# Reading two ids straight from device memory, and issuing their factors ahead of the small vectors and of x

## The chip, the cores and the metric

The kernel runs on one core of a Trainium2 chip. The metric is the device time of one execution in microseconds; three runs of the kernel before are given. A core has five engines with queues of their own: TensorE (PE, with its weight loads PEld), VectorE (DVE), ScalarE (ACT), GpSimd (POOL) and SyncE (SP). DMAs are issued here from the queues of SP and ACT (SPq, ACTq in the profile), and once from that of GpSimd.

## What is computed

x is 8 batches of 256 tokens of 128 features. Each batch has an expert id (0 to 7) and a language id (0 to 3). Cut to what matters:

```python
# first half, x: (8, 256, 128)
h = relu(x @ wi.T + 2 * lora(x; common) + 2 * lora(x; experts[id]))      # 128 -> 512
y = h @ wo.T + 2 * lora(h; common) + 2 * lora(h; experts[id])            # 512 -> 128
for r in range(4):                                                       # 4 rounds
    cw = softmax of the two largest of 4 gate logits (cur @ Wg[r] + bg[r])
    cur = cur + sum_e cw[e] * (gelu(cur @ W1[e] + b1[e]) @ W2[e] + b2[e])
x = x + cur
# second half
z = lora(x; language id) + embed[language id]
x = x + w3(gelu(h2(gelu(h1(silu(w1 z) * (w2 z))))))                      # each with a scale per row
```

## The kernel before

Tokens run along the free dimension, features along the partitions: x is (128, 2048), cut into four chunks of 512 tokens, two batches each. Every fp32 operand is split into a high and a low part of type fp32r, and a product is three matmuls (line 503: high x high, high x low, low x high).

The first stage makes, for each batch, its own weights: the common and the expert's factors are multiplied on TensorE (`merge_group`, lines 511 to 530), VectorE adds twice the product to the base weights (`merged_sum`, line 1029), ScalarE makes the high part (line 798), GpSimd or VectorE the low part (lines 417 and 1034). Kind 0 is the input matrix, kind 1 the output matrix. The factors of a batch are 64 rows of `lora_all`, picked by its id. Then `cond_hidden` and `cond_out` apply the merged weights batch by batch; then come four rounds of 16 expert steps, and the second half.

How the start is ordered. All orders are written out by hand, one program per engine, with semaphores between them.

- SP (line 345): it loads the 16 ids into SBUF (`ids`, line 346), then the small vectors (`vec`, line 347, and the gate bias `gbias`, line 348). It waits for the ids, reads the id of batch 0 into a register (line 244), and issues the two halves of batch 0's factors (`first_load`, line 257); then in the same way the whole factors of batch 2 (`lora_load`, line 247), x of chunk 1 (line 262), batches 4 and 5, x of chunks 2 and 3, batches 6 and 7, the mixture's weights (line 361) and the language factors.
- ACT (lines 893 to 901): base weights of kind 0 (line 265), x of chunk 0 (line 262), a small activation that brings in its table (line 896), a wait for the ids, the factors of batch 1 (`first_load`) and of batch 3 (`lora_load`), base weights of kind 1; then `x0_high(0)` (line 876), the high part of chunk 0's x, and the high parts of the merged weights.
- VectorE (from line 1217): `split_gate`, which waits for both small vectors (line 1200) and splits the gate's weights in four operations (lines 1201 to 1209); `x0_low(0)` (line 1016), which waits for x0_high(0); the sums (0,0) and (1,0), `first_low` (line 1034), the sums (0,1), (1,1), (2,0), (3,0), (2,1), (3,1) (batch, kind).
- TensorE (from line 673): 13 warm-up matmuls on a zero tile (line 590), merge_group 0 (batches 0 and 1, kind 0; waits for the first halves of their factors) and 1 (the same batches, kind 1; second halves), two more warm-up matmuls, merge_group 2 and 3 (batches 2 and 3), cond_hidden(0), cond_hidden(1), and so on.

A PSUM bank is written again only after VectorE's sum has read it: merge_group 3 writes the banks of the sums (0,0) and (1,0), and cond_hidden(1) the banks of the sums (2,0) and (3,0). An fp32 matmul shows as two instructions in the profile, so the 13 warm-up matmuls are 26 rows.

Of the kernel before, what the change touches and what calls it, by code (L numbers as in the profile page):

```python
# [31 lines left out]
LORA_EXPERTS, LANGS = 8, 4  # L32
# [79 lines left out]
def adaln_ffn(nc, x_t, batch_ids, cond_base, lora_all, lang_lora, lang_embed,  # L112
              moe_w, vecs, gate_bias, ffn_w, out_t):
    ctx = ExitStack()
    with ctx:
        def sb(name, shape, dt):
            return ctx.enter_context(nc.sbuf_tensor(name, shape, dt))
# [31 lines left out]
        ids = sb("ids", [1, 2 * BATCHES], I32)  # L149
# [73 lines left out]
        def lora_rows(b, kind):  # L223
            first = 2 * RANK * (2 * (b % 2) + kind)
            return slice(first, first + 2 * RANK)
# [15 lines left out]
            return max([SUMS.index(MERGED[i]) + 1 for i in range(k) if merge_bank(i) == at], default=0)  # L241

        def lora_expert(queue, b):
            return queue.value_load(ids[0:1, b:b + 1], min_val=0, max_val=LORA_EXPERTS - 1)  # L244

        def expert_load(queue, b, e):
            queue.dma_start(lora[4 * RANK * (b % 2):4 * RANK * (b % 2 + 1), b // 2, :],
# [2 lines left out]
        def lora_load(queue, b):  # L250
            expert_load(queue, b, lora_expert(queue, b))

        def first_load(queue, b):

            e = lora_expert(queue, b)
            for kind, arrived in enumerate((lora_in[b], first_out_in[b])):
                queue.dma_start(lora[lora_rows(b, kind), 0, :],  # L257
                                lora_all[bass.ds(e, 1), 2 * RANK * kind:2 * RANK * (kind + 1), :]
                                .rearrange("e r n -> (e r) n")).then_inc(arrived, 16)

        def x_load(queue, c):
            queue.dma_start(x0[:, c, :], x_t[:, c * CHUNK:(c + 1) * CHUNK]).then_inc(x_in[c], 16)

        def base_load(queue, kind):
            queue.dma_start(base[:, kind, :], cond_base[:, kind, :]).then_inc(base_in[kind], 16)
# [42 lines left out]
        def out_parts(c):  # L308

            parts = 2 if c == CHUNKS - 1 else 1  # L310
            return [slice(i * CHUNK // parts, (i + 1) * CHUNK // parts) for i in range(parts)]
# [25 lines left out]
        def store_out(queue, c, t):  # L337
            queue.dma_start(out_t[:, c * CHUNK:(c + 1) * CHUNK][:, t], x0[:, c, t]).then_inc(out_done, 16)
# [5 lines left out]
        @block.sync  # L344
        def _(sp):
            sp.dma_start(ids[:], batch_ids).then_inc(ids_in, 16)
            sp.dma_start(vec[:], vecs).then_inc(small_in, 16)
            sp.dma_start(gbias[:], gate_bias.to_broadcast([SQ, ROUNDS * EXPERTS])).then_inc(small_in, 16)  # L348
            sp.wait_ge(ids_in, 16)
            first_load(sp, 0)  # L350
            lora_load(sp, 2)
            x_load(sp, 1)
            for b in (4, 5):
                lora_load(sp, b)
            for c in (2, 3):
                x_load(sp, c)
            for b in (6, 7):
                lora_load(sp, b)
            for i in (0, 2, 1, 3):
                half = slice((i % 2) * 2 * F, (i % 2 + 1) * 2 * F)  # L360
                sp.dma_start(moe_raw[:, i // 2, half], moe_w[:, i // 2, half]).then_inc(moe_in[i], 16)
            for b in range(BATCHES):
                e = sp.value_load(ids[0:1, BATCHES + b:BATCHES + b + 1], min_val=0, max_val=LANGS - 1)
                sp.dma_start(lang_f[b // 4][:, b % 4, :],
                             lang_lora[bass.ds(e, 1), :, :].rearrange("e r n -> (e r) n")).then_inc(lang_in, 16)
                sp.dma_start(emb[:, b:b + 1],
                             lang_embed[bass.ds(e, 1), :].rearrange("e d -> d e")).then_inc(lang_in, 16)

            def store_gate(slot, turned, read, stored):

                sp.wait_ge(cw_turned, turned)
                if read is not None:
                    sp.wait_ge(cw_ready[slot], read)
                sp.dma_start(cw_dram[slot:slot + 1, :].rearrange("s (e t) -> (s e) t", t=CHUNK),
                             cw_row[0:EXPERTS, :])\
                  .then_inc(cw_stored, 16)
                sp.wait_ge(cw_stored, stored)

            def broadcast_gate(slot):

                sp.dma_start(cw_all[:, slot, :, :].rearrange("p e t -> p (e t)"),
                             cw_dram[slot:slot + 1, :].to_broadcast([P, EXPERTS * CHUNK])).then_inc(cw_ready[slot], 16)

            for slot in range(2):
                store_gate(slot, slot + 1, None, 16 * slot + 16)
                sp.wait_ge(moe_lo_done, max(MOE_ORDER.index(EXPERTS * slot + e) for e in range(EXPERTS)) + 1)
                broadcast_gate(slot)
            with sp.Fori(1, ROUNDS * CHUNKS // 2) as pair:

                read = sp.to_reg(16 * pair)  # L390
                counts = [(sp.to_reg(2 * pair + slot + 1), sp.to_reg(32 * pair + 16 * slot + 16),
                           sp.to_reg(2 * EXPERTS * pair + EXPERTS * (slot - 1) + ADD0)) for slot in range(2)]
                for slot, (turned, stored, gated) in enumerate(counts):
                    store_gate(slot, turned, read, stored)
                    sp.wait_ge(add_done, gated)
                    broadcast_gate(slot)
            for c in range(CHUNKS - 1):
                sp.wait_ge(evac_done, Z_ALL + c + 1)
                store_out(sp, c, slice(0, CHUNK))
            sp.wait_ge(out_done, 16 * sum(len(out_parts(c)) for c in range(CHUNKS)))  # L400
# [391 lines left out]
        def _(act):  # L792
# [98 lines left out]
                   .then_inc(moe_hi_done, 1)  # L891

            base_load(act, 0)
            x_load(act, 0)
            act.wait_ge(const_done, 1)
            act.activation(low_any[0:1, :], blank[0:1, 0:1], ACT.Gelu_apprx_tanh)
            act.wait_ge(ids_in, 16)
            first_load(act, 1)
            lora_load(act, 3)
            base_load(act, 1)  # L900
            x0_high(0)
# [460 lines left out]
```

## Time and profile before

| | us |
|---|---|
| three runs: median (lowest, highest) | 484.4 (484.19, 484.8) |
| span of the profiled execution, first to last instruction | 482.6 |
| median less that span | 1.8 |
| TensorE busy | 477.5 |
| ScalarE busy | 393.6 |
| VectorE busy | 387.7 |
| GpSimd busy | 116.9 |

The profile is that of one execution; its own time with what lies around the span isn't listed, so the span is set beside the median of the runs. A row of the timeline gives the start and the length in us, the engine, the line of the kernel, the operation, the tile written and the tiles read, how many instructions are merged in the row, and in brackets the idle time of the engine just before it with what ended it. A row marked SPq or ACTq is an instruction of a queue's sequencer, such as the issue of a DMA. The landing of a DMA is counted from the start of its issue. The granted clock of TensorE is 1.00 in every stretch that the profile lists.

### The profile page before, as it was taken

The numbers are of one execution on the slowest core, as the hardware profiler recorded it, in microseconds if no ns is written. First come the engines' busy times: TensorE is split into PE (matmuls) and PEld (weight loads), VectorE is DVE, ScalarE is ACT, GpSimd is POOL, SyncE is SP. The second block draws the span as 40 slices with busy tenths as digits, with TensorE's granted clock in tenths as the row PEclk, the third lists the DMA queues.
The fourth block names the chain that finished last, engine by engine and source line by source line (L and its number), as shares of the span: only waits on it lengthen the run. The fifth ranks groups of instructions, "written<-read, shape, count | busy, mean of one in ns | idle before, by whom it ended". The sixth has DMA issues, their size and how long they took to land.

```text
span 482.6 us, 7478 instructions
## 1 busy us (share of the span) xinstructions
PE 477.5 (99%) x2270; PEld 396.2 (82%) x2270; DVE 387.7 (80%) x641; ACT 393.6 (82%) x542; POOL 116.9 (24%) x99
## 2 busy tenths in 40 slices
PE   8999999999999999999999999999999999999997
PEld 7998888888888888888888888888888887888886
DVE  4889899998889898988898898889897658554343
ACT  4889988888788898888888888888888888697653
POOL 3995212121212212121212121231313144400000
PEclk9999999999999999999999999999999999999999
DMA  7702702020210202020202112120202000000002
GB/s 206 219 6 90 282 2 89 0 90 1 88 52 35 88 0 88 0 88 0 88 1 87 37 50 87 45 89 0 88 2 88 2 0 0 1 0 1 0 22 70
DMA packets 7179, 26.31 MB, mean 55 GB/s; under 512 B 2226, under 2 KB 2610, under 8 KB 4978
## 3 DMA queue, kind: packets, MB, share of 16 engines
q1 hardware_dynamic: 5970, 21.73, 12.8%
q0 software_dynamic: 288, 2.88, 1.6%
q10 hardware_dynamic: 896, 1.38, 1.0%
q8 instruction: 14, 0.23, 0.2%
q14 instruction: 11, 0.09, 0.1%
HBM read 24.81 MB, written 1.18 MB: 54 GB/s over the span
## 4 chain that ended last, share of the span: by engine, by line
PE 97%; DMA 1%; SPq 1%; DVE 0%; issue 0%
PE bank L505 34%; PE bank L506 34%; PE bank L509 26%; PE bank L594 1%; PE bank L595 1%; DMA stage<-lora_all 1%; PE bank L527 1%; PE bank L524 0%; SPq L244 0%; PE bank L540 0%; SPq L257 0%; DVE act_out L1029 0%; DVE stage L1029 0%; DVE x L1280 0%; SPq L348 0%
## 5 line engine op out<-in xcount | busy, mean ns | idle before, releaser
L812 ACT ACTIVATE act_out<-bank,vec 128x512 f32<-128x512 f32 x256 | 165.4, 682 | 41.7 <-PE bank L509 32.2
L1119 DVE TENSOR_TENSOR hid_lo<-act_out,hid_hi 128x1024 fp32r<-128x1024 f32 x128 | 156.7, 1243 | 33.2 <-ACT hid_hi L817 33.1
L817 ACT ACTIVATE hid_hi<-act_out 128x1024 fp32r<-128x1024 f32 x128 | 135.9, 1062 | 8.0 <-PE bank L509 0.2
L468 POOL TENSOR_TENSOR cur<-cur,prod 128x512 f32<-128x512 f32 x48 | 64.9, 1353 | 237.1 <-DVE prod L1130 236.6
L505 PE MATMUL bank<-hid_hi,moe_hi 128*128 128x512 f32 x256 | 99.9, 390 | 0.0
L505 PE MATMUL bank<-xhi,moe_hi 128*128 128x512 f32 x256 | 99.7, 390 | 0.0
L509 PE MATMUL bank<-hid_hi,moe_lo 128*128 128x512 f32 x256 | 99.7, 390 | 0.0
L506 PE MATMUL bank<-hid_lo,moe_hi 128*128 128x512 f32 x256 | 99.7, 389 | 0.0
L506 PE MATMUL bank<-xlo,moe_hi 128*128 128x512 f32 x256 | 99.6, 389 | 0.0
L509 PE MATMUL bank<-xhi,moe_lo 128*128 128x512 f32 x256 | 99.6, 389 | 0.0
L505 PEld LDWEIGHTS bank<-hid_hi,moe_hi 128*128 128x128 f32 x256 | 48.1, 188 | 11.3 <-issue 0.2
L509 PEld LDWEIGHTS bank<-hid_hi,moe_lo 128*128 128x128 f32 x256 | 48.1, 188 | 10.2
L506 PEld LDWEIGHTS bank<-hid_lo,moe_hi 128*128 128x128 f32 x256 | 48.1, 188 | 10.1
L509 PEld LDWEIGHTS bank<-xhi,moe_lo 128*128 128x128 f32 x256 | 48.0, 188 | 10.0
L505 PEld LDWEIGHTS bank<-xhi,moe_hi 128*128 128x128 f32 x256 | 48.1, 188 | 10.0
L506 PEld LDWEIGHTS bank<-xlo,moe_hi 128*128 128x128 f32 x256 | 48.1, 188 | 9.9
L1130 DVE SCALAR_TENSOR_TENSOR prod<-bank,vec,cw_all 128x512 f32<-128x512 f32 x64 | 47.5, 742 | 0.2 <-PE bank L509 0.2
L505 PE MATMUL bank<-hid_hi,ffn_hi 128*128 128x512 f32 (+1 forms) x108 | 37.8, 353 | 0.0
L506 PE MATMUL bank<-hid_lo,ffn_hi 128*128 128x512 f32 (+1 forms) x108 | 37.4, 350 | 0.0
L999 ACT ACTIVATE act_out<-bank,vec 128x512 f32<-128x512 f32 x32 | 21.3, 685 | 14.5 <-PE bank L506 14.3
L505 PE MATMUL bank<-xhi,ffn_hi 128*128 128x512 f32 (+1 forms) x84 | 29.8, 355 | 0.5 <-DVE act_out L1029 0.5
L506 PE MATMUL bank<-xlo,ffn_hi 128*128 128x512 f32 (+1 forms) x84 | 29.3, 349 | 0.0
(125 smaller groups left out, 566.3 us busy)
## 6 DMA issues: line engine op xcount, KB each, us to landing
cw_all<-cw_dram SPq DMA_DIRECT2D x16, 1024.0 KB, 4.7
stage<-ffn_w POOLq DMA_DIRECT2D x1, 2304.0 KB, 8.6
cw_all<-moe_w SPq DMA_DIRECT2D x4, 512.0 KB, 7.8
stage<-lora_all SPq DMA_DIRECT2D x5, 160.0 KB, 3.7
x<-x_t SPq DMA_DIRECT2D x3, 256.0 KB, 4.3
out_t<-x SPq DMA_DIRECT2D x3, 256.0 KB, 2.5
cur<-cond_base ACTq DMA_DIRECT2D x2, 256.0 KB, 3.3
stage<-ffn_w POOLq DMA_DIRECT2D x1, 512.0 KB, 4.0
```

What stands on the lines that cost most here:

```text
L468: pool.tensor_tensor(cur[:, c, :], cur[:, c, :], prod[:, s % 2, :], ALU.add).then_inc(add_done, 1)
L505: pe.matmul(out, w_hi, r_hi, start=start, stop=False)
L506: mm = pe.matmul(out, w_hi, r_lo, start=False, stop=stop and w_lo is None)
L509: return pe.matmul(out, w_lo, r_hi, start=False, stop=stop)
L527: mm = pe.matmul(bank[:, at, fc * D:(fc + 1) * D], factors[:, fc * P:(fc + 1) * P], factors[:, F:F + D], start=True, stop=True)
L594: pe.matmul(bank[0:SQ, at, :], wg_now[:], xhi[:, c, :], start=True, stop=False)
L595: pe.matmul(bank[0:SQ, at, :], wg_now[:], xlo[:, c, :], start=False, stop=True).then_inc(logit_done, 1)
L812: act.activation(act_out[:, f // 2, f % 2, :], bank[:, f, :], ACT.Gelu_apprx_tanh, bias=vec[:, V_B1 + e * FC + f:V_B1 + e * FC + f + 1]).t ...
L817: act.activation(hid_hi[:, s % 2, 2 * pr:2 * pr + 2, :], act_out[:, pr, :, :], ACT.Copy)\
L999: act.activation(act_out[:, o // 2, o % 2, :], bank[:, o + FC * (at % 2), :], ACT.Gelu, scale=vec[:, v + o:v + o + 1]).then_inc(gelu_done, 1)
L1119: dve.tensor_tensor(hid_lo[:, s % 2, 2 * pr:2 * pr + 2, :], act_out[:, pr, :, :], hid_hi[:, s % 2, 2 * pr:2 * pr + 2, :].bitcast(F32), ALU ...
L1130: dve.scalar_tensor_tensor(prod[:, s % 2, :], bank[:, 4 + s % 2, :], vec[:, V_B2 + e:V_B2 + e + 1], cw_all[:, c % 2, e, :], ALU.add, ALU.m ...
```

## The change

The id of batches 0 and 1 is read into a register from the input tensor in device memory, not from its copy in SBUF, so that this read needs no wait. SP issues batch 0's factors right after the ids' own transfer, ahead of `vec` and `gbias`, and ACT issues batch 1's ahead of x of chunk 0. All other ids are still read from SBUF after the wait. Bytes, transfers and arithmetic are the same.

```diff
         def lora_expert(queue, b):
-            return queue.value_load(ids[0:1, b:b + 1], min_val=0, max_val=LORA_EXPERTS - 1)
+
+            where = batch_ids if b < 2 else ids
+            return queue.value_load(where[0:1, b:b + 1], min_val=0, max_val=LORA_EXPERTS - 1)
...
         @block.sync
         def _(sp):
             sp.dma_start(ids[:], batch_ids).then_inc(ids_in, 16)
+            first_load(sp, 0)
             sp.dma_start(vec[:], vecs).then_inc(small_in, 16)
             sp.dma_start(gbias[:], gate_bias.to_broadcast([SQ, ROUNDS * EXPERTS])).then_inc(small_in, 16)
             sp.wait_ge(ids_in, 16)
-            first_load(sp, 0)
             lora_load(sp, 2)
             x_load(sp, 1)
...
             base_load(act, 0)
+            first_load(act, 1)
             x_load(act, 0)
             act.wait_ge(const_done, 1)
             act.activation(low_any[0:1, :], blank[0:1, 0:1], ACT.Gelu_apprx_tanh)
             act.wait_ge(ids_in, 16)
-            first_load(act, 1)
             lora_load(act, 3)
             base_load(act, 1)
             x0_high(0)
```

## Rows read from the trace of the kernel before

**Rows 1.** The page: the span, and busy time with its share of it.

```profile
span 482.6 us, 7478 instructions
PE 477.5 (99%) x2270; PEld 396.2 (82%) x2270; DVE 387.7 (80%) x641; ACT 393.6 (82%) x542; POOL 116.9 (24%) x99
```

**Rows 2.** Stretches: length, TensorE busy (instructions), granted clock, DMA share, GB/s.

```profile
8.00:12.30 4.30, 3.65 (x36) 1.00 0.87 251
...
50.00:470.00 420.00, 419.97 (x1859) 1.00 0.12 45
```

**Rows 3.** Waits of TensorE over the span: us in total, times, longest.

```profile
PE bank L505 <- DVE act_out L1029: 0.5, 1, 0.5
PE bank L524 <- DMA stage<-lora_all: 0.2, 1, 0.2
```

**Rows 4.** Timeline of TensorE, 0 to 14 us: start, length, line, operation.

```profile
1.06 5.45 PE L590 MATMUL bank<-blank 128*128 128x128 f32 x26 [1.06 <-POOL blank L405]
6.44 0.70 PE L524 MATMUL bank<-stage 32*128 32x512 f32 x2
...
9.02 1.16 PE L527 MATMUL bank<-stage 32*128 32x128 f32 x16
...
12.29 0.36 PE L505 MATMUL bank<-xhi,ffn_hi 128*128 128x256 f32 x1 [0.50 <-DVE act_out L1029]
```

**Rows 5.** Timeline of VectorE, 0 to 14 us.

```profile
4.84 0.17 DVE L1201 COPY wg_raw<-vec 128x16 f32<-128x16 f32 x1 [4.84 <-DMA gbias<-gate_bias]
...
5.52 0.18 DVE L1209 CAST wg_now<-wg 128x32 fp32r<-128x32 f32 x1
6.41 0.69 DVE L1016 TENSOR_TENSOR xlo<-x,xhi 128x512 fp32r<-128x512 f32 x1 [0.71 <-ACT xhi L876]
7.67 1.29 DVE L1029 SCALAR_TENSOR_TENSOR prod<-bank,cur 128x512 f32<-128x512 f32 x2 [0.57 <-PE bank L527]
...
11.47 0.68 DVE L1029 SCALAR_TENSOR_TENSOR act_out<-bank,cur 128x512 f32<-128x512 f32 x1
```

**Rows 6.** Timeline of ScalarE and its queue, 0 to 14 us.

```profile
1.25 0.45 ACTq L262 DMA_DIRECT2D x<-x_t  x1
...
2.92 0.37 ACTq L257 DMA_DIRECT2D stage<-lora_all  x1
...
5.11 0.59 ACTq L265 DMA_DIRECT2D cur<-cond_base  x1
5.75 0.63 ACT L876 ACTIVATE xhi<-x 128x512 fp32r<-128x512 f32 x1 [2.52 <-issue]
```

**Rows 7.** Timeline of SP's queue, 0 to 14 us.

```profile
0.81 0.36 SPq L346 DMA_DIRECT2D ids<-batch_ids  x1
...
1.65 0.42 SPq L348 DMA_DIRECT2D gbias<-gate_bias  x1
3.09 0.85 SPq L257 DMA_DIRECT2D stage<-lora_all  x2
4.71 0.58 SPq L247 DMA_DIRECT2D stage<-lora_all  x1
```

**Rows 8.** Register loads, line 244: ns min/median/max, first and last start.

```profile
L244 SPq TENSOR_LOAD <-ids x6: 268/273/480, 2.1 to 10.9; - x6
...
L244 ACTq TENSOR_LOAD <-ids x2: 287/380/472, 2.0 to 3.8; - x2
```

**Rows 9.** DMA issues, 0 to 6 us: count, KB each, median us to landing.

```profile
x<-x_t ACTq DMA_DIRECT2D x1, 256.0 KB, 3.3
...
stage<-lora_all SPq DMA_DIRECT2D x2, 80.0 KB, 2.3
...
stage<-lora_all SPq DMA_DIRECT2D x1, 160.0 KB, 3.7
vec<-vecs SPq DMA_DIRECT2D x1, 26.5 KB, 2.6
...
gbias<-gate_bias SPq DMA_DIRECT2D x1, 2.0 KB, 3.1
```

## The prediction

> **What bounds the kernel now.** I read the page first. TensorE is busy for 477.5 of 482.6 us [rows 1], so the reader should look for the few microseconds in which it isn't, and ask what ends them. The stretches say where they are: from 8 to 12.3 us TensorE works 3.65 of 4.30 us, and from 50 to 470 us 419.97 of 420.00 us [rows 2]. The list of TensorE's waits names two in the stage that the change touches: 0.2 us for factors that a DMA brings (batches 2 and 3), and 0.5 us for VectorE's sum at line 1029, before the matmul at 12.29 [rows 3, 4]. Nothing later on TensorE waits, so whatever moves 12.29 moves the end by the same amount: there is no slack behind it to swallow a delay, nor anything that adds to a gain.
>
> Then I followed 12.29 backwards on VectorE. It runs `merged_sum(0,0)` at 7.67 and from there works back to back: seven operations, the last the sum of (3,0), 11.47 to 12.15 [rows 5]. cond_hidden(1) needs that sum because it frees the PSUM bank that it writes. The merge at 9.02 (batches 2 and 3, second kind) hangs on the same chain: it needs the banks that the first two sums free, and starts when the second of them ends, 7.67 + 1.29 = 8.96 [rows 4, 5]. So the number that sets the end is the start of VectorE's first sum, 7.67. It waits for two things: the product on TensorE, and VectorE's own earlier work in program order, `split_gate` and `x0_low(0)`, which ends at 6.41 + 0.69 = 7.10 [rows 5]. TensorE was last, by 0.57 us. And TensorE's first merge starts at 6.44 because the 26 halves of the 13 warm-up matmuls run from 1.06 to 6.51 (ends are modelled) [rows 4].
>
> The factors of batches 0 and 1, which the change hurries, were there by then: SP issues its two from 3.09 to 3.94, the second at about 3.6, and each lands 2.3 us after its issue, at 5.4 and 5.9 [rows 7, 9]. Their time isn't on the path; the warm-up hides it by 0.5 us.
>
> **What the change does, part by part.** Call the time of a register load from device memory X. No row of before shows one. The nearest rows are the same load from SBUF, 0.27 to 0.48 us [rows 8], a floor, and from above the smallest landing of a DMA out of device memory that is listed, 2.3 us [rows 9]. Between them lies the ids' own transfer: issued at 0.81, and ACT's load of it starts at 2.0 [rows 7, 8], so the 64 bytes came from device memory into SBUF within 1.2 us. A direct load makes the read trip but not the write and its semaphore. I take X = 1.1, near that row, and keep 0.48 and 2.3 for the range.
>
> The first row that bears on the price is again that SBUF load of at most 0.48 us [rows 8]. The Trainium skill, DMA: Bandwidth & Descriptors, section on latency and other measured facts, gives a floor of about 600 ns for a tensor_load; by that figure the sum below would be 0.5 us lower. No row of before shows it.
>
> *Removed:* the two early factor loads no longer wait for `ids`. Gain: the first factor DMA of SP is issued at 1.22 + X + 0.5 = 2.8 in place of 3.09 (1.22 is where the next issue begins after ids, 0.81 + 0.36 and 0.05 between; 0.5 is 3.09 less the end of today's load, 2.1 + 0.48) [rows 7, 8]. On ACT likewise. Worth 0.3 us of arrival and, behind the warm-up, nothing at the end.
>
> *Moved past on SP:* one register load, its range check and two DMA issues now stand ahead of `vec` and `gbias`. The two issues take 0.85 us [rows 7]. gbias, issued at 1.65 today, is issued at 1.22 + X + 0.5 + 0.85 + 0.47 = 3.04 + X = 4.1 (0.47: vec's issue and gap, 1.22 to 1.65 and the gap ahead of it). Behind gbias VectorE's `split_gate` waits, and behind that, in order, x0_low(0) and all sums. Today gbias lands at 1.65 + 3.1 = 4.75, VectorE starts at 4.84, ends split_gate at 5.52 + 0.18 = 5.70 and would be free for the first sum 0.65 us of x0_low later: 1.65 us from landing to readiness, 6.40, so 1.27 us of slack [rows 5, 9]. After, with L for the landing, it is ready at 4.69 + X + L, against 7.67: a delay of X + L - 2.98. L is 3.1 if it stays as it is, 2.6 as for vec, 2.3 as for the first factors [rows 9]. ACT's x transfer is queued near it in both kernels, base's is over sooner; I take 2.85, between gbias's own and vec's. Delay: 1.1 + 2.85 - 2.98 = 0.97 us.
>
> *Moved past on ACT:* chunk 0's x is issued at 1.25 today; after, behind load and two issues, at 1.26 + X + 0.45 + 0.85 + 0.04 = 2.60 + X (0.45 from the end of ACT's load today, 2.0 + 0.47, to 2.92; the two issues as on SP) [rows 6 to 8]. It lands 3.3 us later, 5.90 + X; x0_high and x0_low follow (5.75 to 6.41 today, then 0.65), so VectorE is ready at 5.90 + 0.04 + X + 0.66 + 0.65 = 7.25 + X [rows 5, 6, 9]. Delay: X - 0.42 = 0.7 us. This runs beside the other and isn't added. Today ACT's x0_high starts at 5.75, when the second base issue (5.11 + 0.59) ends, over a microsecond after x landed [rows 6, 9]: there lies the slack that this eats first.
>
> *The later queue:* the factors of batch 2, issued at 4.71 today, go at 4.25 + X = 5.3 (gbias's issue ends at 3.46 + X; load, check and address 0.79). They land 0.6 us later, at 9.0 instead of 8.4, and TensorE's wait there grows; but the next merge can't start before 9.02 plus the delay of the sums, 10.0, so it is covered, as long as it slips less than VectorE does. base's second half, batch 3, x of chunks 1 to 3, ids 4 to 7 and the mixture's weights slip by the same 0.6 or so. Today TensorE waits for none of them [rows 3], and a slip of 0.6 us is less than the delay of their users. The table load and constant on ACT run beside the queue.
>
> **The sum.** Gain 0, delay the larger of 0.97 and 0.68, so 1.0 us. Against the profiled span: 482.6 + 1.0 = 483.6 us. Its own whole time is not listed; the median of the three runs, 484.4, is 1.8 us over the span, for what lies around it. Forecast: 485.4 us.
>
> **Rivals.** (1) *The load is quick or the small transfers land quicker in a less busy moment.* X near 0.5 and L at 2.3 give a negative X + L - 2.98; x's path gives X - 0.42 = 0.1; so 0 to 0.7 us, about 484.7. For it: vec and gbias no longer queue behind base's 256 KB. Against it: x's 256 KB now go out just ahead of them. Here the kernel is not measurably slower. The skill's 600 ns, as an estimate, would fall in this case.
> (2) *The load is slow.* X from 1.5 to 2.3 gives a delay of 1.4 to 2.3 us, 485.8 to 486.7. For it: the first load from SBUF took 0.48 where later ones took 0.27, so first touches cost something [rows 8]. Against it: the whole ids trip took 1.2.
> (3) *The other side: the merge is bound by the factors, not by the warm-up.* The ends of matmuls are modelled, and the factors land only 0.5 us ahead of 6.44. If in most executions the warm-up ends before 5.9, an earlier arrival lets TensorE's product end sooner. VectorE's own work in today's order ends at 7.10, so the first sum could start 0.57 us sooner at most: 483.8 us. It decides from the point where both delays above turn negative, X + L under 2.98 and X under 0.42; at the floor of 0.27 for X, x's path leaves 0.15 us, and more only if x lands faster too. Against it: no wait of TensorE for those factors is listed [rows 3].
> (4) *The change doesn't do what it says:* the load from device memory could be built as a transfer and a load, and then gains no lead and costs a wait; that is (2) by its price. The order of the issues is the program's own here, so nothing can undo it.
>
> **Chances.** The forecast's own case, a delay of 0.7 to 1.4 us with VectorE late: 0.50. (1) 0.27, (2) 0.15, (3) 0.08. A measurement of this kernel tells about 0.2% from no change, 0.97 us: the bound is 485.4, in the middle of my likeliest case. Slower by over 0.2%: half or a little more of the forecast's case and all of (2), 0.45. Within: the other half, (1) and most of (3), 0.50. Faster by over 0.2%: (3) with a gain that the traces don't offer, 0.05. The range leaves out the tails of (2) and (3): 484.2 to 486.6.
>
> **What would show it.** In the changed profile the load's row at line 244 or its new line gives X; DVE's first row (4.84 today) should start near 7.1, its x0_low near 8.0, the first sum near 8.6, and TensorE's matmul of 12.29 near 13.3 with a wait of about 1.5 us for VectorE in place of 0.5; the first merge should stay at 6.44. The stretch from 50 to 470 us must be unchanged. The prediction is wrong if the first merge starts earlier, if DVE's first sum still starts at 7.7, or if X is outside 0.5 to 2.3 us.

## The result: slower, and by more than forecast

| | before | after |
|---|---|---|
| runs, median (lowest, highest) | 484.42 us (484.19, 484.80), 6 runs | 488.78 us (486.78, 490.13), 6 runs |
| span of the profiled execution | 482.6 us | 487.6 us |
| its mean granted TensorE clock | 1.000 | 0.993 |

The ratio is 1.0085, with a 95% interval of 1.0071 to 1.0099. The forecast was 485.4 us in a range of 484.2 to 486.6: the sign held, and the size was four times too small. One thing stands out before any row is read. The six runs of before lie within 0.6 us, those of after within 3.4 us, and they sort by the granted clock of each run: the two with 0.999 took 486.78 and 487.21 us, the one with 0.996 took 488.36, and the three with 0.992 or 0.993 took 489.21 to 490.13. So there are two amounts to explain, 2.4 to 2.8 us that even the runs at full clock have, and up to 3 us that the clock adds.

The page of after, the span and the busy times, as in [rows 1]:

```profile
span 487.6 us, 7481 instructions
PE 481.3 (99%) x2270; PEld 398.8 (82%) x2270; DVE 387.6 (79%) x641; ACT 394.0 (81%) x542; POOL 116.7 (24%) x99
```

TensorE runs the same 2270 instructions and is busy 3.8 us longer. The stretches of after say where, beside [rows 2] and this one of before:

```profile
12.30:18.00 5.70, 5.70 (x48) 1.00 0.91 260
```

```profile
8.00:12.30 4.30, 2.73 (x26) 0.93 0.91 264
12.30:18.00 5.70, 5.70 (x36) 0.50 0.86 242
20.00:50.00 30.00, 30.00 (x242) 1.00 0.18 57
50.00:470.00 420.00, 419.97 (x1858) 1.00 0.13 47
```

From 50 us on TensorE works as before, at the same clock. From 8 to 12.3 TensorE works 2.73 us where it worked 3.65. From 12.3 to 18 it is busy throughout in both, but at half the clock, 1.2 in place of 2.4 GHz, and gets through 36 instructions where before had 48. By 19 us the loss is complete. The merge that started at 13.89 in before starts 5.17 us later, and the span ends 5.0 us later:

```profile
13.89 0.70 PE L524 MATMUL bank<-stage 32*128 32x512 f32 x2
```

```profile
19.06 0.70 PE L526 MATMUL bank<-stage 32*128 32x512 f32 x2
```

The register loads of after, all at the line that reads the id (line 244 of before, [rows 8]); `batch_ids_ptr` is a word that nobody wrote in the kernel:

```profile
L246 SPq TENSOR_LOAD <-ids x5: 273/277/459, 5.3 to 12.3; - x5
...
L246 SPq TENSOR_LOAD <-batch_ids_ptr x1: 1269/1269/1269, 1.2 to 1.2; - x1
L246 ACTq TENSOR_LOAD <-batch_ids_ptr x1: 1037/1037/1037, 1.2 to 1.2; - x1
...
L246 ACTq TENSOR_LOAD <-batch_ids x1: 471/471/471, 2.4 to 2.4; - x1
L246 SPq TENSOR_LOAD <-batch_ids x1: 476/476/476, 2.5 to 2.5; - x1
```

A read from device memory is two loads in a row: first the address of the tensor, 1.27 us on SP, then the id, 0.48 us. Started at 1.22 they end at 2.99; before, the single load from SBUF ended at 2.6, ids transfer and all. The queue of SP and the timeline of VectorE in after, beside [rows 7] and [rows 5]:

```profile
3.49 0.86 SPq L259 DMA_DIRECT2D stage<-lora_all  x2
4.39 0.42 SPq L350 DMA_DIRECT2D vec<-vecs  x1
4.86 0.43 SPq L351 DMA_DIRECT2D gbias<-gate_bias  x1
6.23 0.58 SPq L249 DMA_DIRECT2D stage<-lora_all  x1
```

```profile
9.29 0.18 DVE L1203 COPY wg_raw<-vec 128x16 f32<-128x16 f32 x1 [9.29 <-DMA gbias<-gate_bias]
...
10.06 0.68 DVE L1018 TENSOR_TENSOR xlo<-x,xhi 128x512 fp32r<-128x512 f32 x1
10.67 1.28 DVE L1031 SCALAR_TENSOR_TENSOR prod<-bank,cur 128x512 f32<-128x512 f32 x2
```

The factors that were to be early go out at 3.49, 0.4 us later than the 3.09 of before. The lead that the change was made for isn't there: the first halves of batch 0's factors land at about 5.5 us, as in before, and the last second half at 7.6 instead of 5.9, which is TensorE's wait of 0.5 us at line 529 below. gbias goes out at 4.86 instead of 1.65, VectorE starts at 9.29 instead of 4.84, and the first sum at 10.67 instead of 7.67: 3.0 us. TensorE's waits in after, beside [rows 3], and how long the transfers took from issue to landing, beside [rows 9]:

```profile
PE bank L526 <- DMA stage<-lora_all: 1.6, 1, 1.6
...
PE bank L529 <- DMA stage<-lora_all: 0.5, 1, 0.5
```

```profile
x<-x_t ACTq DMA_DIRECT2D x1, 256.0 KB, 4.6
...
gbias<-gate_bias SPq DMA_DIRECT2D x1, 2.0 KB, 4.3
```

x took 4.6 us instead of 3.3 and gbias 4.3 instead of 3.1. The list of waits names batch 2's factors, not VectorE. That gave two theories to part. Theory A, the prediction's: VectorE's first sum sets the end. Theory B: the factors of batches 2 and 3 do, as the waits say.

### The profile page after: what moved, and what is told of

Read it like the earlier page. It is cut to its first block, busy times and chain, and to the rows that moved or that the text cites. A ratio compares the mean times of both kernels' runs of the same rounds, so it can differ in the third digit from the quotient of the medians.

```text
span 487.6 us, 7481 instructions
## 1 busy us (share of the span) xinstructions
PE 481.3 (99%) x2270; PEld 398.8 (82%) x2270; DVE 387.6 (79%) x641; ACT 394.0 (81%) x542; POOL 116.7 (24%) x99
## 4 chain that ended last, share of the span: by engine, by line
PE 97%; DMA 1%; SPq 1%; issue 0%; DVE 0%
PE bank L507 34%; PE bank L508 34%; PE bank L511 26%; DMA stage<-lora_all 1%; PE bank L529 1%; PE bank L596 1%; PE bank L597 1%; SPq L246 1%; PE bank L526 0%; PE bank L542 0%; SPq L259 0%; DVE x L1282 0%; SPq L351 0%; SPq L350 0%; SPq L348 0%
## 5 line engine op out<-in xcount | busy, mean ns | idle before, releaser
L508 PE MATMUL bank<-xlo,ffn_hi 128*128 128x512 f32 (+1 forms) x84 | 30.3, 360 | 0.0
```

The source lines that it names most:

```text
L508: mm = pe.matmul(out, w_hi, r_lo, start=False, stop=stop and w_lo is None)
```

## The experiments

Shifts of the first sum are against 7.67, shifts of the span against the 482.6 us of before's profile. The kernel before, run beside them on the same chip, had a median of 484.02 us beside the first four kernels, 484.41 beside the four on the freed VectorE, the longer warm-up, the late gbias and the price of the read, and 484.3 beside the other three (the late gbias with its gap filled, and the two tries). Each experiment was profiled once, and times of rows are those of that one execution.

**Only the source of the ids.** Order as before.

```diff
-            return queue.value_load(ids[0:1, b:b + 1], min_val=0, max_val=LORA_EXPERTS - 1)
+            where = batch_ids if b < 2 else ids
+            return queue.value_load(where[0:1, b:b + 1], min_val=0, max_val=LORA_EXPERTS - 1)
```

> The order of the kernel before, only the ids of batches 0 and 1 are read from device memory. The profile of the changed kernel has two loads for such an id, 1.27 and 0.48 us on SP. They stand in place of one of 0.48, so everything behind them on SP goes 1.3 us later: batch 0's factors at 4.4, batch 2's at 6.0, landing at 9.7. gbias (lands 4.75) and chunk 0's x (issued 1.25) are as before. Theory A (VectorE's first sum sets the end, through gbias and x): the factors of batches 0 and 1 land at 6.7 to 7.2, behind the warm-up's 6.44, and ACT's queue holds x0_high to about 7.0; first sum at 8.4, 0.75 us later, 485.2 us. Theory B (TensorE's wait for the factors of batches 2 and 3 sets the end): the merge of 8.41 goes to 9.7, 485.7 us.

488.11 us, ratio 1.0081 (1.0058 to 1.0104). Both theories missed: 4.1 us for the source alone, and four of the five runs had a granted clock of 0.999 or 1.000, so it isn't the clock. The pointer took 1.77 us on SP and 1.86 on ACT this time. Everything behind it on both queues went about 2 us later, the second base transfer to 7.35 us, and that one landed 6.2 us after its issue. The profiled run is the slowest of the five, 491.18 us at a clock of 0.992, and its span is 6.8 us over before. VectorE's and TensorE's waits in it show who was last:

```profile
13.57 0.69 DVE L1030 SCALAR_TENSOR_TENSOR stage<-bank,cur 128x512 f32<-128x512 f32 x1 [1.99 <-DMA cur<-cond_base]
```

```profile
16.20 0.35 PE L506 MATMUL bank<-xhi,ffn_hi 128*128 128x256 f32 x1 [2.58 <-DVE act_out L1030]
```

The first sum was only 1.8 us late (9.51), but the third waited 2.0 us for the base weights of kind 1, and the matmul of 12.29 started at 16.20, 3.9 us late. The four runs at full clock are 3.5 to 3.9 us of span over before, which is the size of this wait; the other 2.9 us of the profiled run fell behind it, at the lower clock. The chain is VectorE's, as in theory A, yet it can be held in its middle as well as at its head.

**Only the order.** Ids from SBUF, after a wait for their transfer, ahead of vec, gbias and x. The cut is against after; the line that reads the id takes `ids` again.

```diff
             sp.dma_start(ids[:], batch_ids).then_inc(ids_in, 16)
+            sp.wait_ge(ids_in, 16)
             first_load(sp, 0)
             sp.dma_start(vec[:], vecs).then_inc(small_in, 16)
...
             base_load(act, 0)
+            act.wait_ge(ids_in, 16)
             first_load(act, 1)
             x_load(act, 0)
```

> The order of the changed kernel, but both ids are read from SBUF after a wait for the ids' transfer, as in the kernel before. This takes the pointer load (1.27 us) away and puts a wait for a transfer of 1.2 us in its place: first factor DMA at about 3.0, gbias at 4.35 instead of 4.86, batch 2's factors at 5.6 instead of 6.23. If the order is the main cost (theory A), the first sum is still at about 10.1 (10.67 in the changed kernel, 7.67 before) and the time 486.8 to 488.5 us; if the source of the id were the main cost, it would be back within 0.5 us of the kernel before, 484.4 to 484.9 us.

488.36 us, ratio 1.0086 (1.0055 to 1.0118), as expected of the order. First sum at 10.54. The first factors went out at 3.00, 0.5 us earlier than in after: waiting for the copy in SBUF was quicker than reading the id directly. gbias went out at 4.36, 0.5 us earlier than in after, and landed 4.7 us later, 0.4 us slower; the gain in issue time was nearly all lost in the transfer. Each half of the change, the source and the order, costs by itself about as much as both. What they have in common is that both hold the two queues early on: here until about 3 us, with vec, gbias and x still to be issued, and in the source-only run from about 2.1 to 4.9 us, with the factors, the second base transfer and x0_high behind.

**Only ACT's half.** Against before; batch 1's id is read from device memory.

```diff
             base_load(act, 0)
+            first_load(act, 1)
             x_load(act, 0)
...
             act.wait_ge(ids_in, 16)
-            first_load(act, 1)
             lora_load(act, 3)
```

> Only ACT's half of the change: batch 1's id from device memory, its factors ahead of chunk 0's x. SP is as before. gbias lands at 4.75 and batch 2's factors at 8.4 as before. Theory A: x is issued at 4.2 and lands 3.3 to 4.6 us later, 7.5 to 8.8, so the first sum is at 8.8 to 10.1, 1.2 to 2.4 us later: 485.6 to 486.8 us, set by x. Theory B (factors of batches 2 and 3 set the end): batch 3's go at 5.6 instead of 4.5, so about 1.1 us later: 485.5 us, and the row of TensorE's wait names that DMA.

487.61 us, ratio 1.0070 (1.0047 to 1.0093), 0.8 us above the top of what was expected. First sum at 10.41, held by x, issued at 4.20 and landed 4.9 us later. This run shows most clearly what the late x does to others. SP's queue runs as in before, batch 2's factors are issued at 4.71 in both, and yet they took 4.8 us to land and not 3.7, and batch 3's, issued at 5.6, took 5.4:

```profile
4.71 0.58 SPq L249 DMA_DIRECT2D stage<-lora_all  x1
```

```profile
PE bank L526 <- DMA stage<-lora_all: 3.2, 1, 3.2
```

The 256 KB of x, which before went out in the first microseconds, now go out at the same time as the factors, the second base transfer and x of chunk 1. The run doesn't part the two theories: TensorE's next merge starts with those factors at 11.18, and the second sum ends at 10.41 + 1.28 = 11.69, so the merge behind it is held by both within a tenth.

**Only SP's half.** Against before; batch 0's id is read from device memory.

```diff
             sp.dma_start(ids[:], batch_ids).then_inc(ids_in, 16)
+            first_load(sp, 0)
             sp.dma_start(vec[:], vecs).then_inc(small_in, 16)
...
             sp.wait_ge(ids_in, 16)
-            first_load(sp, 0)
             lora_load(sp, 2)
```

> Only SP's half: batch 0's id from device memory, its factors ahead of vec and gbias. ACT is as before, so chunk 0's x lands at about 4.6 and x0_high starts at 5.75. Theory A: gbias is issued at 4.86 and lands 3.1 to 4.3 us later, so the first sum is at 9.6 to 10.8, 1.9 to 3.1 us later: 486.3 to 487.5 us, more where TensorE's granted clock falls. Theory B: batch 2's factors, issued at 6.2, land at 9.9 to 10.9, the merge of 8.41 moves by 1.5 to 2.5 us: 485.9 to 486.9 us, with TensorE's wait on that DMA. A gbias landing near 3.1 us would say that the 4.3 of the changed kernel came from x's transfer beside it.

487.19 us, ratio 1.0063 (1.0038 to 1.0088), inside theory A's numbers and 0.3 us above theory B's. gbias landed in 3.3 us and x in 3.2: with ACT's queue as in before they cost about what they did there. In all profiles with a late gbias it goes by this: with x late it landed in 4.3 us (after), 4.7 (order only), 4.1 (split_gate later) and 4.2 (longer warm-up, below), with x early in 3.3 here and in 3.4 and 3.2 (the two runs with gbias alone late, below). So of the 4.3 us in after, about 1 us came with the later ACT queue. x's 256 KB are the likely part of it, but batch 3's factors and the second base transfer are later with them, and no run moves x alone. First sum at 9.91, 2.2 us late, as theory A had it; this profile is of a run at 0.996. The one run at clock 1.000 took 486.26 us, a span of 484.4, 1.8 us over before; it wasn't profiled.

**VectorE freed from gbias.** The changed kernel, with split_gate later.

```diff
-            split_gate()
             x0_low(0)
...
             relu_low(0)
+            split_gate()
             merged_sum(4, 0)
```

> The changed kernel, with VectorE's split_gate (the four operations that wait for vec and gbias) moved behind relu_low(0). So the late gbias holds nothing any more. Theory A: the first sum then waits for chunk 0's x alone: landed at 8.8, x0_high, x0_low, first sum at 10.1 instead of 10.67; TensorE's next merge follows, and the time at full granted clock falls by 0.4 to 0.6 us, from 486.8 to 487.2 to 486.3 to 486.7. Theory B (batch 2's factors, landed at 11.0, set the end): no change. If the first sum is earlier and the end is not, both bind within a few tenths.

The first sum moved to 9.83, 0.84 us earlier than in after, and the matmul that was at 12.29 started at 14.45, 2.16 us late as the first sum was, behind a wait of 0.5 us for VectorE as in before. With gbias out of the way x alone holds the sum, so x's path costs 2.16 us. But the end didn't gain: 488.88 us, ratio 1.0101 (1.0081 to 1.0120), and 485.8 us of span at full clock, not below the 485.0 and 485.5 of after. The four operations cost 0.9 us at their old place and 2.2 us at the new one, from 16.55 to 18.79, just ahead of the sums that TensorE needs next:

```profile
16.55 0.52 DVE L1203 COPY wg_raw<-vec 128x16 f32<-128x16 f32 x1
17.10 1.27 DVE L1206 CAST wg<-wg_raw 128x128 fp32r<-128x128 f32 x1
18.40 0.18 DVE L1208 TENSOR_TENSOR wg<-wg_raw,wg 128x16 fp32r<-128x16 f32 x1
```

The merge at 16.04 was still 2.15 us late, the next, at 20.64, waited 0.4 us for a sum and was 2.60 late, and the span ends 3.2 us later. So this run confirms the chain up to 16 us; behind that its edit brought a cost of its own.

**The clock.** The changed kernel with more warm-up matmuls where TensorE idles.

```diff
-WARM, KEEP_WARM = 13, 2
+WARM, KEEP_WARM = 13, 9
```

> The changed kernel with 9 instead of 2 warm-up matmuls between the merges of batches 0 and 1 and those of 2 and 3. They add some 1.6 us of work on a zero tile into TensorE's idle time from 9.4 to 11.0. Clock theory: of the six runs of the changed kernel the two with a mean granted clock of 0.999 took 486.8 and 487.2 us, the others 488.4 to 490.1. If that idle time is what lets the clock fall, all runs are now at 0.999 or above and take 486.6 to 487.3 us. If the clock falls for another reason, the spread of the changed kernel stays, median near 488.8.

487.60 us, ratio 1.0085 (1.0054 to 1.0117). Three of the four runs were at 1.000 and took 487.14, 487.35 and 487.84 us; the fourth was at 0.991 and took 490.18. Less than expected, since one run still fell; with four runs here and six of after the shift in how often it falls is likely, not shown. The profiled run is the clean one to read, because its clock is 1.000: first sum at 10.59, +2.92 us; the matmul of 12.29 at 15.20, +2.91; span 485.4, +2.8. At full clock the delay passes to the end one for one.

**gbias late, and nothing else.** The kernel before with one issue moved; ids from SBUF, no factor issued later than before.

```diff
             sp.dma_start(vec[:], vecs).then_inc(small_in, 16)
-            sp.dma_start(gbias[:], gate_bias.to_broadcast([SQ, ROUNDS * EXPERTS])).then_inc(small_in, 16)
             sp.wait_ge(ids_in, 16)
             first_load(sp, 0)
             lora_load(sp, 2)
+            sp.dma_start(gbias[:], gate_bias.to_broadcast([SQ, ROUNDS * EXPERTS])).then_inc(small_in, 16)
             x_load(sp, 1)
```

> The kernel before with one issue moved: gbias goes out behind the factors of batches 0 and 2 instead of ahead of them, at about 4.9 us instead of 1.65. Ids come from SBUF, x and all factors go at their old times or 0.4 us earlier. Theory A: gbias lands 3.1 to 4.3 us later, at 8.0 to 9.2, the first sum is at 9.6 to 10.8 and the time 486.0 to 487.1 us, more where the clock falls. Theory B: the factors arrive as before or earlier, so 484.0 to 484.4 us.

489.35 us, ratio 1.0103 (1.0079 to 1.0128). A transfer of 2 KB in the wrong place costs as much as the whole change. TensorE had batch 2's factors at 8.58 and then waited for VectorE:

```profile
8.58 1.13 PE L524 MATMUL bank<-stage 32*128 32x512 f32 x4 [0.26 <-DMA stage<-lora_all]
11.43 2.08 PE L527 MATMUL bank<-stage 32*128 32x128 f32 x16 [1.72 <-DVE prod L1029]
```

The first sum was at 10.09. Theory B, which asked for 484.0 to 484.4, falls. But theory A's 486.0 to 487.1 is short too, by 1 to 3 us, and here its clause on the clock is what counts: all four runs had a granted clock of 0.991 to 0.996, and from 12.3 to 18 us it was 0.50:

```profile
12.30:18.00 5.70, 5.70 (x33) 0.50 0.94 249
```

**The same, with TensorE kept busy in that wait.**

```diff
             merge_group(2)
+            warm(8)
             merge_group(3)
```

> The kernel before with gbias issued behind the factors of batches 0 and 2 (as in the run with the late gbias: first sum at 10.09 instead of 7.67, 486.4 to 488.4 us of span, mean granted clock 0.991 to 0.996), and with 8 warm-up matmuls between the merges of kind 0 and kind 1 of batches 2 and 3, where TensorE then waits 1.7 us for VectorE. If the delay of the first sum passes to the end one for one and the rest of that run's loss is the clock's: granted clock 0.999 or more, span 482.6 + 2.4 = 485.0, 486.8 us. If the loss has another cause besides, the time stays at 488 to 490 us at full clock.

487.42 us over nine runs (486.77 to 488.33), ratio 1.0064 (1.0047 to 1.0081); eight of the nine at 1.000, one at 0.998. The profiled run of 486.77 us has its first sum at 9.88, +2.2 us, and a span of 485.0, +2.4. The added matmuls are work on a zero tile, and they give back 1.9 us of median:

```profile
9.42 2.05 PE L590 MATMUL bank<-blank 128*128 128x128 f32 x16
11.40 1.16 PE L527 MATMUL bank<-stage 32*128 32x128 f32 x16
```

Without them the 16 instructions of that merge took 2.08 us, with them 1.16. This is the second term: with TensorE idle for 1.7 us ahead of them the granted clock fell in four runs of four, with that stretch filled it stayed at 0.998 or above in nine of nine, and the work behind ran at the higher level. The median is 0.6 us above the expected 486.8, so not all of the rest is the first sum.

**The price of the read by itself.** Every batch id from device memory, order as before.

```diff
-            return queue.value_load(ids[0:1, b:b + 1], min_val=0, max_val=LORA_EXPERTS - 1)
+            return queue.value_load(batch_ids[0:1, b:b + 1], min_val=0, max_val=LORA_EXPERTS - 1)
```

> The order of the kernel before, but every batch id is read from device memory, six times on SP and twice on ACT: the price of such a read at different loads of the DMA engines, and whether the pointer is loaded each time. So far it took 1.04 and 1.27 us for the pointer plus 0.47 for the value when issued at 1.2 us, and 1.86 and 1.77 plus 0.47 at 2.1 us with transfers under way. If the pointer is loaded again each time: six loads of 1.0 to 1.9 us on SP; if busy DMA engines make it dear, those from 5 to 12 us take the longest, near 1.8. The kernel is 3 to 6 us slower than before.

```profile
L244 SPq TENSOR_LOAD <-batch_ids_ptr x6: 909/1074/1748, 2.1 to 18.7; - x6
L244 SPq TENSOR_LOAD <-batch_ids x6: 462/468/625, 3.9 to 20.0; - x6
```

490.11 us in its single run. The pointer is loaded again for every read, 0.91 to 1.75 us on SP, the value 0.46 to 0.63; the two reads on ACT are pairs too. The dearest were those at 2.1 us (1.75), with the DMA engines 88% busy from 2 to 4 us, and at 9.3 (1.67), with 39% from 8 to 10; those at 5.8, 12.7 and 16.2 took 0.91 to 1.01, with 23%, 30% and 68%, and that at 18.7 took 1.14. Busy engines may make it dear, but not in step with their share, and the forecast of 1.8 us for all from 5 to 12 us missed.

**Two tries at a faster kernel.** If the sums set the end, VectorE should do first those that TensorE awaits. Edits to the kernel before; the high and low parts of chunk 1's x also go one place earlier, which the cut leaves out:

```diff
-SUMS = ((0, 0), (1, 0), (0, 1), (1, 1), (2, 0), (3, 0), (2, 1), ...
+SUMS = ((0, 0), (1, 0), (2, 0), (3, 0), (0, 1), (1, 1), (2, 1), ...
...
-            merged_sum(0, 1)
-            merged_sum(1, 1)
             merged_sum(2, 0)
             merged_sum(3, 0)
+            merged_sum(0, 1)
+            merged_sum(1, 1)
```

> The kernel before with VectorE's sums (2,0) and (3,0) ahead of (0,1) and (1,1), and the high part (ScalarE) and low part (GpSimd) of x of chunk 1 one place earlier. cond_hidden(1) waits 0.5 us at 12.29 for the sum of (3,0), which then ends 1.2 us sooner, at 10.95. Theory A, that TensorE's waits on VectorE's sums set the end one for one: cond_hidden(1) starts at 11.8 behind cond_hidden(0), and the time is 0.4 to 0.5 us less, 483.9 us. If the sums that now come later (0,1 and 1,1) are awaited in turn by cond_out(0), near 15 us, it is the same or slower, 484.4 us or more.

The second try adds x0_high(0) ahead of ACT's second base transfer and moves one warm-up matmul:

```diff
-            base_load(act, 1)
             x0_high(0)
+            base_load(act, 1)
...
-WARM, KEEP_WARM = 13, 2
+WARM, KEEP_WARM = 12, 3
```

> The version with the sums reordered, and besides x0_high(0) ahead of the second base transfer on ACT, so that it starts when x has landed and its queue is free (5.1 instead of 5.75), and one warm-up matmul moved from before the first merge to the two behind it (12 and 3). VectorE would be ready for the first sum at 6.45 instead of 7.1, the merge would start at 6.0 to 6.2 instead of 6.44, behind the second half of the factors that lands at 5.9: first sum at about 7.3 instead of 7.67, together 0.7 to 0.9 us less than before, 483.5 to 483.7 us. Rival: the merge waits for the factors and the granted clock, so nothing more than the reordering gives.

Both are slower: 488.80 us, ratio 1.0089 (1.0059 to 1.0119), and 488.65 us, ratio 1.0077 (1.0050 to 1.0103); so are their runs at a clock of 1.000, 487.41 and 487.27 us. The wait of 12.29 was gone, as meant, and larger ones stood behind it. From the waits of TensorE in the first:

```profile
PE bank L524 <- DVE fifth L1029: 2.6, 1, 2.6
...
PE bank L505 <- POOL ffn_lo L417: 0.5, 1, 0.5
```

The place in SUMS also decides which of six scratch tiles a sum goes to, and a later sum waits until GpSimd has made the low part of the one in its tile; VectorE waited 1.2 and 2.6 us for that. The order of the sums is tied to GpSimd's order, and I had changed the one without the other. No version found here beats the kernel before.

## Why the prediction was wrong, step by step

**That nothing is to be gained: right.** The first merge of after starts at 5.98, right behind a warm-up that ended sooner; it waited for no factor. The hoped-for lead didn't come either: the prediction had SP's first factor DMA at 2.8 us, and it went at 3.49, behind 3.09 of before. In the run with the late gbias and in the second try TensorE waited 0.2 to 0.3 us for the first factors, so rival (3) is real in some executions, but it is worth tenths of a microsecond.

**The chain: right, and shown.** The end follows VectorE's first sum: +2.92 us there and +2.8 at the end in the run with the longer warm-up, +2.2 and +2.4 in the late gbias with its gap filled. gbias alone was enough. No run delays the factors of batches 2 and 3 alone, so what they would cost by themselves stays open. The prediction expected TensorE's wait at the matmul of 12.29 to grow from 0.5 to 1.5 us; it can't, since the merge ahead of it moves with the same sums, and with the longer warm-up it was 0.5 again. A second correction: the source-only run shows a second place where the chain can be held, the base weights of kind 1 ahead of the third sum. The prediction dismissed a slip of that transfer as smaller than the delay of its users; with a slip of 2.2 us and a landing of 6.2 us it was the larger.

**X: mis-sized, 1.77 for 1.1.** The prediction priced one load. There are two, pointer then value. The nearest row that it leaned on, the ids' own transfer of 1.2 us, prices a trip by a DMA engine and not that of a sequencer. Rival (2), 1.5 to 2.3, had X right, with a chance of only 0.15, and its time of 485.8 to 486.7 was still short. The rule cited from the Trainium skill, DMA: Bandwidth & Descriptors, section on latency and other measured facts, of about 600 ns, doesn't fit here: a single load went below it, 0.27 us from SBUF and 0.46 for the value, and the whole read, being two loads, took 1.5 us in its cheaper case in after (1.04 + 0.47 on ACT) and 2.3 in the source-only run.

**L: mis-sized, 4.3 for 2.85. This is the larger miss, 1.5 us.** The step that failed is the sentence that ACT's x transfer is queued near it in both kernels. It was near it, but what else was under way had changed. From 3 to 4.2 us the DMA share was 0.92 in before; in after, with both sequencers in their register loads until 3 us, it was 0.01 (first before, then after):

```profile
3.00:4.20 1.20, 1.20 (x7) 1.20 (x7) 0.00 (x0) 0.21 (x2) 0.00 (x0) 1.00 0.92 250
```

```profile
3.00:4.20 1.20, 1.20 (x7) 1.20 (x7) 0.00 (x0) 0.00 (x0) 0.00 (x0) 1.00 0.01 3
```

The columns are the length, the busy time of PE, PEld, DVE, ACT and POOL, the granted clock, the DMA share and GB/s. What wasn't moved then was moved later: while gbias was under way, from 5.6 to 6.9 us, the queues issued another 832 KB (two sets of factors, the second base transfer, x of chunk 1), besides the 256 KB of x just ahead of it. That this is what held gbias and x is argued from these rows and from the run with only SP's half, not shown by a run of its own. With X and L as measured, the prediction's own formula, X + L - 2.98, gives 1.77 + 4.3 - 2.98 = 3.1 us; the first sum was 3.0 late. The formula stood, its two inputs didn't. x's path, beside it, was mis-sized for the same reasons: 0.7 us in the prediction, with a landing of 3.3 us, and 2.16 us in the run with split_gate later, with one of 4.3.

**The covered slip: a narrow escape.** Batch 2's factors slipped by 2.6 us (8.41 to 11.02) and not by 0.6. The next merge started at 12.00, right at the end of the second sum at 11.95, so the cover held by about 0.4 us, if the factors alone would have let that merge start at 11.02 + 0.61 (before's distance from 8.41 to 9.02). That is why the list of waits names them: they were last for one merge, VectorE for the next.

**The clock: not in the sum at all.** The prediction said that TensorE's wait would grow and asked nothing of what a longer wait does. It costs next to nothing in some runs of after and up to 3 us in others, and the profiled one has 5.17 - 3.0 = 2.2 us of it. In the medians it is 4.4 (488.78 - 484.42) less the 2.4 to 2.8 of the runs at full clock, so 1.6 to 2.0 us. Even with a right X and L the range would have had to reach some 3 us higher.

Still open: what in a given run decides whether the clock falls. The profiled run with split_gate later had TensorE idle for 1.9 us ahead of the same merge and kept a clock of 1.000, that of after fell with 1.6 us, and one run of the kernel before, beside the last three kernels, had a clock of 0.996 and took 487.88 us among fifteen from 483.56 to 485.00.

## What to carry to other kernels

Before an issue is put first on a queue, ask which waiting instruction stands behind each one that it pushes back, and that a small transfer can head the longest chain. Price every read of device memory into a register as a stall of its queue, here 1.4 to 2.3 us, and a stall of both queues by the bytes that go out later among others, not by the stall alone. And when TensorE's idle time grows near the start, add the work behind it at half clock to the upper end of the range.

## What the runs showed of the hardware

- A register load from a kernel's input tensor is two loads, one behind the other, the tensor's address and the value: 0.91 to 1.86 us and 0.46 to 0.63 us, against 0.27 to 0.48 from SBUF. The address was loaded anew for each of the eight reads.
- The same cast of 128x128 from f32 to fp32r on VectorE took 0.23 us at 5 us and 1.27 us at 17 us, when GpSimd ran a subtraction from 16.99 to 18.28. The Trainium skill, SBUF — State Buffer, section on the two separate sides, states that VectorE and GpSimd share a pair of SBUF ports, held by one of them for a whole instruction. By that rule the cast, started at 17.10 and ended at 18.37, waited for that subtraction, and the numbers agree. So do those of the copy ahead of it, 0.17 us at the old place and 0.52 from 16.55 on, when GpSimd's subtraction from 15.76 to 17.04 was under way. No run here took GpSimd away.
- One merge of 16 instructions took 2.08 us after an idle stretch and 1.16 us behind filler matmuls.
